# Expert layers: products of biases ahead of the tiles, first rows ahead of weights, outputs summed by TensorE

## The chip, the cores and the metric

The kernel runs on one core of one Trainium2 chip. The metric is device time in microseconds (us) of one launch. Before the change it is 1733.27 us, the median of three runs (1730.6 to 1735.8).

## The reference, cut to what matters

A decoder of four layers, each of a self attention, a cross attention and a feed-forward, each followed by a residual sum and a layer norm: `x = layernorm(x + sub(x))`. x has 8 batches of 112 rows of 256 values. The change lies in the feed-forwards of layers 0 and 1, which are mixtures of 8 experts (256 to 1024 to 256). Layer 0 weighs the best two experts of each row:

```python
logits = einsum('bsd,ed->bse', x, w_router)
top_vals, top_idx = top_k(logits, 2)
router_weights = softmax(top_vals)
h = gelu(einsum('eud,bsd->bseu', w_up, x) + b_up)
down = einsum('edu,bseu->bsed', w_down, h) + b_down
out = sum over the two picks of router_weights * down[pick]
```

Layer 1 scales the row by its gate `wi` ahead of expert i, and a row's output is that of the last expert with `wi > 0`, so only one expert's output counts per row:

```python
h = relu(xf * wi @ w1[i] + b1[i])
y = h @ w2[i] + b2[i]
out = where(wi > 0, y, out)
```

## The kernel before, in words

All is f32. The program of each engine is written out by hand, and semaphores order them. SUBS lists the twelve stages; `experts` is the part of stages 2 and 5 on TensorE (`pe`), VectorE (`dve`) and ScalarE (`act`), `expert_tiles` their part on SyncE (`sp`), `routed` theirs on GpSimd (`pool`). n is 0 for the first of these stages ("first layer" below) and 1 for the second ("second layer").

Routing gives each row a slot in DRAM (`slots`), in which rows of one expert stand together; GpSimd sends rows there with indirect DMAs (line 3865, semaphore `sent`), the last two batches of rows at the start of the stage. There are 21 tiles of 128 rows in the first layer and 14 in the second. A small `table` says which expert and which region of `slots` each tile has; SyncE loads both numbers into registers for each tile (`registers`, lines 685 and 686).

Per tile SyncE fetches a block of rows (`rows_to`, xrow, 128 KB), the up-weights (`up_weights`, wup, about 1 MB) and the down-weights (`down_weights`, wdn, 1 MB), three buffers each, and stores the outputs (yrow). Weights of tile 0 are fetched much earlier. For tile i + 3 the block of rows is issued after the down-weights of tile i + 2, which wait until the down-products of tile i - 1 are done. TensorE turns the rows (`turned`, line 2020), multiplies by the up-weights (`up`, line 2031, 32 records) and, after ScalarE's activation (line 2645), by the down-weights (`down`, line 2044, 16 records). A f32 matmul shows as two records. Its order is turned(0), turned(1), up(0), and then for each i: turned(i + 2), up(i + 1), down(i). VectorE copies turned rows and outputs out of the banks (lines 3555, 3571).

The bias of the down-products is not added per tile. For each batch of rows t, one matmul of the transposed gates (wtT) with the eight biases gives what all picks of a row add. `biases(t)` (line 2007) makes this product ahead of turned(t + 2), into the upper half of that tile's bank, and VectorE adds the residual to it (line 3565, into `acc`). So tiles 2 to 9 each carry one.

While TensorE waits for the first rows it runs fillers: `warm` (line 845) is one matmul of 256 columns, two records, whose result is not used. There are eight of them ahead of turned(0).

After the last tile GpSimd fetches each row's outputs back with indirect DMAs (line 4051, ygot: two per batch in the first layer, one in the second). VectorE multiplies them with their gates and adds them to `acc` (lines 3584, 3586; in the second layer one addition, 3589), takes the statistics of the norm (2723, 2726), the reciprocal (3575) and the normed rows (2732). ScalarE takes the root (2654). TensorE turns the normed rows (852), ScalarE copies them out (2171, 2663). `opening(sub, t)` on each engine is what the next stage starts between these batches: on TensorE the queries and keys (line 880, 16 records) at t = 3, the values (888, and a turn 1117 in the first layer) at t = 4, and in the first layer the second queries and keys at t = 5. Three fillers stand ahead of rows_t(6) and three ahead of rows_t(7).

Of the kernel before, what the change touches and what calls it, by code (L numbers as in the profile page):

```python
# [22 lines left out]
ALU = mybir.AluOpType  # L23
# [7 lines left out]
START = 64  # L31
# [126 lines left out]
class Ffn:  # L158
# [10 lines left out]
    Ffn("L0_ffn", dn=8),  # L169
    Turned("L1_attn", rope=True),  # L170
    Cross("L1_xattn", mask=True, joined=True),
    Ffn("L1_ffn", dn=8),
# [71 lines left out]
def decoder(nc, ctxT, mask, mask_keys, x, consts, ffn_small, packs, ring_dram, moe_up, moe_dn, out):  # L244
    ctx = ExitStack()
    with ctx:
# [52 lines left out]
        with ExitStack() as turn:  # L299
# [72 lines left out]
            xs = take(T, B, DM)  # L372
            lg = take(T, B, 8)
# [126 lines left out]
        mix_step = sem("mix_step")  # L500
# [117 lines left out]

        def route_bank(n, k):

            return bank[turn_banks(SUBS[4], "L", k, 0, 0)[1]] if n and k < 4 else bank[0]
# [29 lines left out]
        def _(sp):  # L651
# [25 lines left out]
            def expert_tiles(sub):  # L677
# [154 lines left out]
        def _(pe):  # L832
# [1152 lines left out]
            def experts(sub, router, bias):  # L1985
# [18 lines left out]
                def biases(t):  # L2004

                    g = tile_of(n, t + 2)
                    pe.matmul(bank[g % 2][0:T, DM:2 * DM], wtT[:, t * T:(t + 1) * T], f(bias, 8),
                              start=True, stop=True).then_inc(dn_ready, 1)

                def turned(i):  # L2010
# [37 lines left out]
                for _ in range(8):  # L2048
                    warm(bank[3], 256)
# [3 lines left out]
                for i in range(count):  # L2053
                    if i + 2 < count:
                        turned(i + 2)
                    if i + 1 < count:
                        up(i + 1)
                    down(i)
                for t in range(B):
# [3 lines left out]
                    rows_t(sub, t, t % 2, bank[t % 2])  # L2063
                    opening(sub, t)
# [648 lines left out]
        def _(dve):  # L2713
# [810 lines left out]
            def experts(sub, key):  # L3524
# [32 lines left out]

                turned_in(0)
                turned_in(1)
                for i in range(count):  # L3560
                    if i + 2 < count:
                        turned_in(i + 2)
                    if i < B:
                        dve.wait_ge(dn_ready, db + i + 1)
                        dve.tensor_tensor(acc[:, i, :], bank[tile_of(n, i) % 2][0:T, DM:2 * DM], x_res[:, i, :], ALU.add)\
                            .then_inc(dn_done, 1)
# [10 lines left out]
                mixed = Steps(dve, mix_step, 0, B)  # L3577
                for t in range(B):
                    if t >= 2:
                        dve.wait_ge(xln_ready, at(sub, "row", t - 2, 1))  # L3580
                        apart(dve)
                    dve.wait_ge(got_in[t % 4], 16 * (2 * sum(PICKS[:n]) + PICKS[n] * (t // 4 + 1)))
# [661 lines left out]
```

## Time and profile before

| what | value |
|---|---|
| median of three runs | 1733.27 us (1730.6 to 1735.8) |
| the profiled execution's own time | 1736.08 us |
| its span | 1734.3 us |
| mean granted clock of TensorE | 0.961 |
| busy: TensorE matmul, VectorE, ScalarE, GpSimd | 1529.8, 881.5, 646.6, 412.1 us |
| tiles of the first layer | about 364 to 526 us in the span |
| tiles of the second layer | about 857 to 968 us in the span |

How to read it: times are us from the start of the span, durations us unless marked ns. PE is TensorE's matmul and PEld its weight loads (which overlap), DVE is VectorE, ACT ScalarE, POOL GpSimd, SP SyncE; SPq and the like are an engine's queue. L2031 is line 2031 of the kernel. The granted clock is a share of 2.4 GHz: 1.00 is 2.4 GHz and 0.50 is 1.2 GHz, its other level. Names are tiles without buffer numbers: `bank` is PSUM, `route` holds acc and wtT, `arena` the routing's scratch among others.

### The profile page before, as it was taken

The page shows a single profiled execution, that of the slowest core. Times are in us where ns is not written, and L with a number is a line of the kernel's source. Part 1 is how long each engine was busy: PE and PEld are TensorE (multiplying, and loading weights), DVE is VectorE, ACT ScalarE, POOL GpSimd, SP SyncE. Part 2 cuts the span into 40 slices and gives each one's busy share as a digit, 9 for nine tenths or more (in the row PEclk, how much of TensorE's full clock was granted, in tenths as well). Part 3 has the DMA queues.
Part 4 walks back from the last instruction along what each step waited for, and adds up shares of the span by engine and source line. Part 5 has one row for each costly group of instructions (what it writes and reads, how often), then busy time and mean ns, then how long its engine had stood idle before and what let it go on. Part 6 is the DMA issues. An engine that isn't in the chain of part 4 may idle for free.

```text
span 1734.3 us, 39360 instructions
## 1 busy us (share of the span) xinstructions
PE 1529.8 (88%) x15024; PEld 1263.2 (73%) x15024; DVE 881.5 (51%) x2278; ACT 646.6 (37%) x1547; POOL 412.1 (24%) x627
## 2 busy tenths in 40 slices
PE   7998998889995888887799599997998999999998
PEld 6876777678994665565588477875786776789897
DVE  3665777521105555556311364567344555666764
ACT  3334876323332333444122323662663444311110
POOL 2224776610004331111100134552111111000101
PEclk9998999989997999999899799998999999999999
DMA  5443000178871002110588201101002000033332
GB/s 201 157 155 137 29 27 15 55 270 299 320 274 49 2 1 83 30 30 7 221 278 301 90 1 47 42 28 49 2 1 76 29 29 2 25 122 98 94 104 67
DMA packets 41984, 166.82 MB, mean 96 GB/s; under 512 B 6114, under 2 KB 16994, under 8 KB 30306
## 3 DMA queue, kind: packets, MB, share of 16 engines
q1 hardware_dynamic: 39522, 159.14, 26.5%
q0 software_dynamic: 2304, 5.51, 1.0%
q8 instruction: 106, 1.74, 0.4%
q14 instruction: 52, 0.43, 0.1%
HBM read 140.22 MB, written 24.41 MB: 95 GB/s over the span
## 4 chain that ended last, share of the span: by engine, by line
PE 67%; DVE 14%; issue 8%; POOL 4%; ACT 3%; DMA 3%; SPq 0%; DVEq 0%; POOLq 0%; ACTq 0%
PE bank L2031 7%; PE bank L2044 7%; PE bank L1973 4%; PE bank L1975 4%; PE bank L1974 4%; PE bank L1638 2%; PE bank L880 2%; PE bank L871 2%; PE bank L1658 2%; PE bank L845 2%; PE bank L1627 2%; PE bank L1401 2%; DVE big L3417 2%; PE bank L972 2%; DMA xrow<-slots 1%
## 5 line engine op out<-in xcount | busy, mean ns | idle before, releaser
L3708 POOL TENSOR_TENSOR mv<-mv,cst 112x1 f32<-112x1 f32 x88 | 20.8, 237 | 586.5 <-DVE mv L2726 586.5
L2645 ACT ACTIVATE htile<-bank,wup 128x128 f32<-128x128 f32 x280 | 79.8, 368 | 188.5 <-PE bank L2031 188.5
L2031 PE MATMUL bank<-xtile,wup 128*128 128x128 f32 x1120 | 135.2, 280 | 0.2
L2031 PEld LDWEIGHTS bank<-xtile,wup 128*128 128x128 f32 x1120 | 132.2, 197 | 1.1 <-DVE xtile L3555 1.0
L2044 PE MATMUL bank<-wdn,htile 128*128 128x256 f32 x560 | 126.3, 379 | 0.0
L3571 DVE COPY yrow<-bank 128x256 f32<-128x256 f32 x35 | 14.9, 425 | 217.2 <-PE bank L2044 217.2
L2044 PEld LDWEIGHTS bank<-wdn,htile 128*128 128x128 f32 x560 | 103.9, 190 | 12.7
L3882 POOL TENSOR_SCALAR arena<-arena,c_lo 112x375 f32<-112x375 f32 x64 | 98.0, 1544 | 33.8 <-ACT c_lo L2416 33.6
L2686 ACT ACTIVATE tmp<-bank,ffs 128x448 f32<-128x448 f32 x48 | 30.5, 635 | 182.8 <-PE bank L1975 182.7
L4051 POOL DMA_INDIRECT ygot<-slots,arena x24 | 22.9, 955 | 310.1 <-DMA slots<-yrow 300.2
L845 PE MATMUL bank<-ffs 128*128 128x256 f32 (+1 forms) x326 | 87.3, 413 | 2.1 <-ACT route L2636 2.1
L3417 DVE CUSTOM_DVE_ANT_0 big<-bank,big 112x375 f32<-112x375 f32 x128 | 62.6, 546 | 51.6 <-PE bank L1638 51.2
L2171 ACT COPY xT<-bank 128x224 f32<-128x224 f32 (+1 forms) x96 | 33.6, 350 | 145.0 <-PE bank L852 139.3
L2509 ACT ACTIVATE arena<-bank,arena 125x448 f32<-125x448 f32 x96 | 53.0, 635 | 79.5 <-PE bank L1658 79.5
L852 PE MATMUL bank<-cst,xln 112*128 112x112 f32 x176 | 37.2, 297 | 51.3 <-DVE xln L2732 44.5
L3420 DVE TENSOR_REDUCE arena<-bank 112x2 f32<-112x750 f32 x64 | 57.2, 936 | 40.2 <-PE bank L1638 40.1
L1638 PE MATMUL bank<-big,arena 32*112 32x375 f32 x512 | 57.6, 517 | 18.7 <-ACT arena L2509 13.5
L2412 ACT ACTIVATE arena<-big,nm 112x375 f32<-112x375 f32 x128 | 70.8, 603 | 8.7 <-DVE nm L3336 7.1
L845 PEld LDWEIGHTS bank<-ffs 128*128 128x128 f32 x326 | 63.3, 203 | 13.3 <-ACT route L2636 2.8
L852 PEld LDWEIGHTS bank<-cst,xln 112*128 112x128 f32 x176 | 22.8, 158 | 68.9 <-DVE xln L2732 53.8
L1401 PEld LDWEIGHTS bank<-cst,arena 112*125 112x125 f32 x384 | 49.5, 194 | 24.2 <-issue 9.1
L2511 ACT ACTIVATE arena<-bank 125x448 f32<-125x448 f32 x96 | 44.5, 550 | 58.9 <-PE bank L1658 58.4
(388 smaller groups left out, 3800.4 us busy)
## 6 DMA issues: line engine op xcount, KB each, us to landing
wup<-in_moe_up SPq DMA_DIRECT2D x35, 1028.0 KB, 7.3
wdn<-in_moe_dn SPq DMA_DIRECT2D x35, 1024.0 KB, 5.6
vspace<-in_ring SPq DMA_DIRECT2D x40, 512.0 KB, 4.1
ctxs<-parts SPq DMA_DIRECT2D x30, 564.0 KB, 3.7
slots<-mlpw SPq DMA_DIRECT2D x11, 1024.0 KB, 6.4
parts<-ctxs SPq DMA_DIRECT2D x8, 564.0 KB, 3.1
xrow<-slots SPq DMA_DIRECT2D x35, 128.0 KB, 4.9
slots<-yrow SPq DMA_DIRECT2D x35, 128.0 KB, 7.1
```

What stands on the lines that cost most here:

```text
L845: pe.matmul(out[:, 0:n], f("rhsT")[:, 0:128], f("rhsT")[:, 0:n], start=True, stop=True)
L1401: mm = pe.transpose(bank[4 + (3 * g + t) % 2][0:KT, j * T:(j + 1) * T], c_pr[:, g, j, t * KT:(t + 1) * KT], ident[0:T, 0:T])
L1638: mm = pe.matmul(out[i][0:T, 0:S2], c_qm[rows, p, g // 2, g % 2, :], c_kT[rows, p, g // 2, :], start=True, stop=True)
L1973: pe.matmul(out, weights[0], rows[0], start=start, stop=False)
L1974: pe.matmul(out, weights[0], rows[1], start=False, stop=False)
L1975: return pe.matmul(out, weights[1], rows[0], start=False, stop=stop)
L2031: mm = pe.matmul(bank[2 + 2 * (g % 2) + m // 4][:, m % 4 * ROWS:(m % 4 + 1) * ROWS], wup[:, g % 3, k * HID + 128 * m:k * HID + 128 * m + 1 ...
L2044: mm = pe.matmul(bank[6 + g % 2][:, 0:DM], htile[:, g % 2, k, :], wdn[:, g % 3, k * DM:(k + 1) * DM], start=(k == 0), stop=(k == 7))
L2412: nc.scalar.activation(c_pr[:, g, j, :], c_sc[:, g % 2, j, :], ACT.Exp, bias=nm[:, p, h:h + 1], scale=-1.0).then_inc(cexp_done, 1)
L2645: ins = nc.scalar.activation(htile[:, g % 2, m, :], bank[2 + 2 * (g % 2) + m // 4][:, m % 4 * ROWS:(m % 4 + 1) * ROWS], func, bias=wup[:, ...
L3417: ins = dve.tensor_tensor_reduce(c_sc[:, g % 2, i, :], bank[first + k][0:T, 0:S2], c_row[:, b % 2, :], 1.0, -LOWEST, ALU.add, ALU.min, j_m ...
L3882: ins = nc.gpsimd.tensor_scalar(c_pr[:, g, j, :], c_pr[:, g, j, :], c_lo[:, p, h:h + 1], 1.0, ALU.max, ALU.min)
```

## The change

- All eight products of biases move to the place ahead of the fillers, into banks that the first up- and down-products don't use yet (`bias_rows`); the fillers go from eight to four. VectorE adds the residual to four of them before its copy of tile 0's rows and to four after it. up(1) waits for all eight additions.
- SyncE now waits for the sends (`sent`) right after the registers of tile 0 and issues rows_to(0), then the registers of tile 1, up_weights(1), rows_to(1), down_weights(1), the registers of tile 2, rows_to(2), up_weights(2), down_weights(2). Before, the registers of all three tiles and both weights of tile 1 went ahead of the wait, and the three blocks of rows followed it together.
- After the last tile, TensorE sums the outputs: per batch it multiplies each ygot block and acc by the identity (in the first layer ygot by a diagonal matrix of gates, `mix`, that VectorE makes during the tiles) and accumulates in a bank, three banks in turn. Three batches go ahead of rows_t(0); the output of batch t + 3 stands between rows_t(t) and opening(t). VectorE reads statistics and normed rows out of that bank.

```diff
@@ expert_tiles (SyncE)
                 registers(0)
+                sp.wait_ge(sent, 16 * B * sum(PICKS[:n + 1]))
+                rows_to(0)
                 registers(1)
                 up_weights(1)
+                rows_to(1)
                 down_weights(1)
                 registers(2)
-                sp.wait_ge(sent, 16 * B * sum(PICKS[:n + 1]))
-                rows_to(0)
-                rows_to(1)
                 rows_to(2)
@@ experts (TensorE)
+                for t in range(B):
+                    pe.matmul(bias_rows(n, t), wtT[:, t * T:(t + 1) * T], f(bias, 8), start=True, stop=True).then_inc(dn_ready, 1)
...
-                    if 4 <= i < B + 4:
-                        pe.wait_ge(dn_done, db + i - 3)
-                    if 2 <= i < B + 2:
-                        biases(i - 2)
...
+                    if i == 1:
+                        pe.wait_ge(dn_done, db + B)
...
-                for _ in range(8):
-                    warm(bank[3], 256)
+                for _ in range(4):
+                    warm(bank[7 - (2 + 2 * (tile_of(n, 1) % 2))], 256)
...
+                def outputs(t):
+
+                    pe.wait_ge(got_in[t % 4], 16 * (2 * sum(PICKS[:n]) + PICKS[n] * (t // 4 + 1)))
+                    if t >= 3:
+                        pe.wait_ge(xln_ready, at(sub, "row", t - 3, 1))
+                    parts = [(mix[:, k, t, :] if n == 0 else ident[0:T, 0:T], ygot[:, t, k, :]) for k in range(PICKS[n])]
+                    parts.append((ident[0:T, 0:T], acc[:, t, :]))
+                    for k, (picks, rows) in enumerate(parts):
+                        mm = pe.matmul(bank[(2, 6, 7)[t % 3]][0:T, 0:DM], picks, rows, start=(k == 0), stop=(k == PICKS[n]))
+                    mm.then_inc(dn_ready, 1)
+
+                pe.wait_ge(edn_done, tile_of(n, count - 1) + 1)
+                for t in range(3):
+                    outputs(t)
                 for t in range(B):
...
                     rows_t(sub, t, t % 2, bank[t % 2])
+                    if t + 3 < B:
+                        outputs(t + 3)
                     opening(sub, t)
@@ experts (VectorE)
+                def biases_in(t):
+
+                    dve.wait_ge(dn_ready, db + t // 2 * 2 + 2)
+                    dve.tensor_tensor(acc[:, t, :], bias_rows(n, t), x_res[:, t, :], ALU.add).then_inc(dn_done, 1)
+
+                for t in range(4):
+                    biases_in(t)
                 turned_in(0)
+                for t in range(4, B):
+                    biases_in(t)
                 turned_in(1)
...
+                    for k in range(2 if n == 0 and i < B else 0):
+                        dve.tensor_scalar(mix[:, k, i, :], c("ident", T)[:, 0:T], gw[:, 1 + k, i:i + 1], None, ALU.mult)
...
-                    if n == 0:
-                        mixed(dve.scalar_tensor_tensor(out=acc[:, t, :], in0=ygot[:, t, 0, :], scalar=gw[:, 1, t:t + 1],
-                                                       in1=acc[:, t, :], op0=ALU.mult, op1=ALU.add))
-                        ins = dve.scalar_tensor_tensor(out=res[:, t % 2, :], in0=ygot[:, t, 1, :], scalar=gw[:, 2, t:t + 1],
-                                                       in1=acc[:, t, :], op0=ALU.mult, op1=ALU.add)
-                    else:
-                        ins = dve.tensor_tensor(res[:, t % 2, :], ygot[:, t, 0, :], acc[:, t, :], ALU.add)
-                    ins.then_inc(ln_dve, 1)
-                    stats(sub, t, t % 2, 0)
+                    stats_of(t)
                     if t:
                         inverse(t - 1)
-                        rows_out(sub, t - 1, (t - 1) % 2)
+                        rows_of(t - 1)
                     opening(sub, t)
```

`stats_of` and `rows_of` are the old steps with the bank in place of `res`.

## Rows read from the trace of the kernel before

**Rows 1.** The page: the chain that ended last, by engine.
```profile
PE 67%; DVE 14%; issue 8%; POOL 4%; ACT 3%; DMA 3%; SPq 0%; DVEq 0%; POOLq 0%; ACTq 0%
```
**Rows 2.** The chain in order of time, first layer: start, duration, what.
```profile
352.80 4.80 DMA slots<-x_res,arena
...
357.77 5.62 DMA xrow<-slots
...
371.93 3.57 PE bank L2031 x32
...
396.80 6.44 DMA xrow<-slots
```
**Rows 3.** Windows of one tile each: engines' busy time, granted clock, DMA share, GB/s.
```profile
420.35:428.35 8.00, 8.00 (x54) 6.96 (x54) 1.18 (x3) 2.28 (x8) 0.00 (x0) 1.00 0.82 296
428.35:435.60 7.25, 7.25 (x53) 6.79 (x52) 0.93 (x3) 2.28 (x8) 0.00 (x0) 1.00 0.95 327
```
**Rows 4.** Timeline, start of the first layer's tiles.
```profile
355.63 5.41 PE L845 MATMUL bank<-ffs 128*128 128x256 f32 x16 [1.03 <-ACT route L2636]
...
357.77 1.38 SPq L707 DMA_DIRECT2D xrow<-slots  x3
...
364.63 6.32 PE L2031 MATMUL bank<-xtile,wup 128*128 128x128 f32 x32
```
**Rows 5.** Windows of the fillers and of the first products, first layer.
```profile
355.60:361.04 5.44, 5.41 (x16) 4.14 (x16) 0.00 (x0) 0.00 (x0) 0.00 (x0) 0.69 0.93 342
...
363.43:370.90 7.47, 7.38 (x37) 6.83 (x37) 0.85 (x2) 2.39 (x5) 0.00 (x0) 0.57 0.67 280
```
**Rows 6.** Timeline, start of the second layer's tiles.
```profile
843.82 5.63 PE L845 MATMUL bank<-ffs 128*128 128x256 f32 x16 [1.03 <-ACT route L2636]
...
848.55 0.35 SPq L693 DMA_DIRECT2D wup<-in_moe_up  x1
...
857.80 5.54 PE L2031 MATMUL bank<-xtile,wup 128*128 128x128 f32 x32
```
**Rows 7.** Windows, same place.
```profile
847.00:849.00 2.00, 2.00 (x9) 1.73 (x8) 0.00 (x0) 0.00 (x0) 0.00 (x0) 0.82 0.00 0
...
853.00:855.00 2.00, 0.00 (x0) 0.00 (x0) 0.00 (x0) 0.00 (x0) 0.00 (x0) 0.89 0.99 414
```
**Rows 8.** Landing of xrow (first layer), wup (to 380), ygot (all), each from its own answer.
```profile
DMA to landing us min/median/max: 3.9/4.8/6.4
...
DMA to landing us min/median/max: 4.8/5.4/7.2
...
DMA to landing us min/median/max: 2.6/2.7/6.1
```
**Rows 9.** Timeline, end of the first layer.
```profile
530.04 0.94 POOL L4051 DMA_INDIRECT ygot<-slots,arena  x1 [0.30 <-issue]
...
532.70 0.48 DVE L3584 SCALAR_TENSOR_TENSOR route<-ygot,arena,route 112x256 f32<-112x256 f32 x1 [6.54 <-DMA ygot<-slots,arena]
...
545.85 3.62 PE L880 MATMUL bank<-xT,wat 128*128 128x112 f32 x16
...
552.73 2.04 PE L880 MATMUL bank<-xT,wat 128*128 128x112 f32 x16
```
**Rows 10.** Timeline, end of the second layer.
```profile
993.12 0.41 PE L852 MATMUL bank<-cst,xln 112*128 112x112 f32 x2
```
**Rows 11.** The chain: six and four records of 256 columns, and SP's first load.
```profile
554.77 1.31 PE bank L845 x6
...
813.30 2.05 PE bank L871 x4
...
845.99 0.45 SPq L685
```
**Rows 12.** One line's instructions: count, duration ns min/median/max, first and last start, forms.
```profile
L2723 DVE BATCH_NORM_STATS2 st<-res x104: 416/427/429, 55.0 to 1727.2; 112x6 f32<-112x256 f32 x104
...
L3565 DVE TENSOR_TENSOR route<-bank,x_res x16: 414/415/417, 372.3 to 920.8; 112x256 f32<-112x256 f32 x16
```

More of the change, by code:

```diff
@@ L168 @@
     Cross("L0_xattn", clip=True),
-    Ffn("L0_ffn", dn=8),
+    Ffn("L0_ffn", dn=16),
     Turned("L1_attn", rope=True),
     Cross("L1_xattn", mask=True, joined=True),
-    Ffn("L1_ffn", dn=8),
+    Ffn("L1_ffn", dn=16),
     Turned("L2_attn"),
@@ L372, in decoder @@
             xs = take(T, B, DM)
+            mix = xs.rearrange("p b n -> p (b n)")[:, 0:2 * B * T].rearrange("p (k t n) -> p k t n", k=2, t=B)
             lg = take(T, B, 8)
@@ L499, in decoder @@
         v_zero = sem("v_zero")
-        mix_step = sem("mix_step")
         rt_ready, rt_step, rt_exp = sem("rt_ready"), [sem("rt_step0"), sem("rt_step1")], sem("rt_exp")
@@ L617, in wait_turn, with bias_rows @@
                 eng.wait_ge(route_in, 6 * (sub.index // 3) + b + 1)
+        def bias_rows(n, t):
+            first = 2 + 2 * (tile_of(n, 1) % 2)
+            return bank[(first, first + 1, 6, 7)[t // 2]][0:T, t % 2 * DM:t % 2 * DM + DM]
         def route_bank(n, k):
@@ L2002, in experts @@
                 count = TILES[n]
[L2004 to L2008, printed above, removed]
+                for t in range(B):
+                    pe.matmul(bias_rows(n, t), wtT[:, t * T:(t + 1) * T], f(bias, 8), start=True, stop=True).then_inc(dn_ready, 1)
                 def turned(i):
@@ L3562, in experts @@
                         turned_in(i + 2)
[L3563 to L3566, printed above, removed]
+                    for k in range(2 if n == 0 and i < B else 0):
+                        dve.tensor_scalar(mix[:, k, i, :], c("ident", T)[:, 0:T], gw[:, 1 + k, i:i + 1], None, ALU.mult)
                     g = tile_of(n, i)
@@ L3575, in inverse, with sums @@
                     dve.reciprocal(mv[:, t % 2, 3:4], mv[:, t % 2, 2:3]).then_inc(ln_pool, 2)
-                mixed = Steps(dve, mix_step, 0, B)
-                for t in range(B):
[L3579 to L3582, printed above, removed]
-                    if n == 0:
-                        mixed(dve.scalar_tensor_tensor(out=acc[:, t, :], in0=ygot[:, t, 0, :], scalar=gw[:, 1, t:t + 1],
-                                                       in1=acc[:, t, :], op0=ALU.mult, op1=ALU.add))
-                        ins = dve.scalar_tensor_tensor(out=res[:, t % 2, :], in0=ygot[:, t, 1, :], scalar=gw[:, 2, t:t + 1],
-                                                       in1=acc[:, t, :], op0=ALU.mult, op1=ALU.add)
-                    else:
-                        ins = dve.tensor_tensor(res[:, t % 2, :], ygot[:, t, 0, :], acc[:, t, :], ALU.add)
-                    ins.then_inc(ln_dve, 1)
-                    stats(sub, t, t % 2, 0)
+                def sums(t):
+                    return bank[(2, 6, 7)[t % 3]][0:T, 0:DM]
@@ new lines, in stats_of, with rows_of @@
+                def stats_of(t):
+                    v = START + 3 * (sub.base["ln"] + t)
+                    dve.wait_ge(dn_ready, db + B + t + 1)
+                    dve.bn_stats(st[:, t % 2, :], sums(t)).then_inc(ln_dve, 2)
+                    dve.wait_ge(ln_dve, v + 2)
+                    apart(dve)
+                    dve.bn_aggr(mv[:, t % 2, 0:2], st[:, t % 2, :]).then_inc(ln_dve, 1)
+                def rows_of(t):
+                    dve.wait_ge(xt_ready, xt_at(sub, t) - 2)
+                    dve.wait_ge(xres_done, at(sub, "row", t, -1))
+                    dve.wait_ge(ln_pool, START + 2 * (sub.base["ln"] + t) + 2)
+                    dve.tensor_scalar(xln[:, t % 2, :], sums(t), mv[:, t % 2, 0:1], mv[:, t % 2, 3:4], ALU.subtract, ALU.mult)\
+                        .then_inc(xln_ready, 1)
@@ L3592, in experts @@
+                for t in range(B):
+                    stats_of(t)
                     if t:
                         inverse(t - 1)
-                        rows_out(sub, t - 1, (t - 1) % 2)
+                        rows_of(t - 1)
                     opening(sub, t)
                 inverse(B - 1)
-                rows_out(sub, B - 1, 1)
+                rows_of(B - 1)
+                dve.sem_inc(dn_done, B)
             def quantised(sub):
```

## The prediction

> **What bounds the kernel now.** I read the page of the profile first: TensorE holds 67% of the chain that ended last [rows 1], so what counts is where TensorE waits and what it does needlessly. Then the chain of waits through both expert stages. Each has three parts. It begins with a wait: first for the rows being sent (4.80 us), then for their coming back (5.62 us) [rows 2]. Then it is TensorE alone, tile after tile, with one wait for rows of 6.44 us among them [rows 2]. It ends, after the last tile, in fetches of the outputs and a norm per batch, mixed with the openings of the next stage. The windows of one tile each show the price of a bias directly: 8.00 us for a tile with one, 7.25 us for the next without, granted clock 1.00 in both, TensorE busy to the end of each and the DMA share at 0.95 or less [rows 3]. So the middle is bound by TensorE. The timelines at both starts show what surrounds the wait: eight fillers, 16 records in 5.41 and 5.63 us, then nothing until rows come [rows 4, 6].
>
> **The biases out of the loop.** Sixteen tiles (eight per layer) lose 8.00 - 7.25 = 0.75 us each [rows 3]: -12.0 us. DVE loses an addition per tile there and gains two small products per tile in the first layer; its busy time in a tile is 1.18 us of 8 [rows 3], so both are free. Up-products of tile 1 now wait for all eight additions; these run while TensorE waits for rows or works on tile 0.
>
> **The biases in the wait, first layer.** TensorE starts at 355.63 and now has eight bias pairs and four filler pairs, 24 records. The mean granted clock over the fillers was 0.69 [rows 5]: 38% of them at 2.4 GHz, about 0.6 us before a fall near 356.2 and the rest after a rise near 359.6, and 1.2 GHz between. A 256-column record takes 1.31/6 = 0.22 us at 2.4 GHz and 2.05/4 = 0.51 us at 1.2 [rows 11]. Some 9 records end by 359.6, the other 15 take 3.2 us: done at 362.8. (The gap is small against the bounds: all 24 at 1.2 GHz would take 12.3 us, all at 2.4 GHz 5.3.) The wait lasted until 357.77 + 5.62 = 363.4, so this is covered.
>
> **Rows ahead of weights, first layer.** Before, three blocks of rows were issued from 357.77 on [rows 4], behind the weights of tile 1, and the first took 5.62 us [rows 2]. Now row block 0 is issued with nothing ahead and should land like a gather, in 2.6 us [rows 8]: 360.1. But TensorE turns block 0 and block 1 before its first up-product, and block 1 still stands behind the up-weights of tile 1. These now move behind the wait for the sends, and behind two register loads (one pair about 1.1 us: in the second layer two pairs fill the time from 845.99 [rows 11] to the issue at 848.55 [rows 6]). So: sends done 357.3 to 357.6, up-weights issued near 359.2, landing 4.8 us later at the least [rows 8], block 1 about 0.3 behind: 364.3. Up-products start at 364.4 instead of 364.63 [rows 4]: -0.2 us. That step taken alone gives almost nothing here; the bounds are +1.0 (a landing near 5.4, the median of up-weights [rows 8]) and -1.5 (sends done 2 us earlier, because no weights share the queues).
>
> **The clock that follows.** Before, TensorE stood idle from 361.0 to 363.4. The mean of 0.57 from there to 370.9 says that it then ran at 1.2 GHz until about 369.9 [rows 5]; the first up-products took 6.32 us [rows 4], the next 3.57 us [rows 2]. Now only the 1.5 us from 362.8 to 364.3 are bare, with a turn in them. In the second layer's pause, which began at 843.82 + 5.63 = 849.45 [rows 6], the clock was still up until about 854.6 (0.89 over 853 to 855 [rows 7]). The bare time is shorter than either pause kept it. I take the full clock: -2.75 us. Bounds: 0 and -2.75.
>
> **The same at the second layer.** SP gets the table at 845.99 [rows 11]; no queue moves a byte from 847 to 849 [rows 7], so the sends were done by 847.2. Block 0 goes out near 847.4, not behind the weights as before; the up-weights of tile 1 near 849.0 instead of 848.55, since one issue stands ahead; block 1 near 849.6. Landing 4.8 after the weights plus 0.3: block 1 at 854.1. Fillers and biases, 24 records from 843.82 with the clock low until 847.7 (0.82 in that window [rows 7]), end at 851.2. So up-products start at 854.5 and not at 857.80 [rows 6]: -3.3 us. There the bare time is 2.6 us; I let the clock fall as before, the set taking its 5.54 us. Bounds: -2.0 (weights landing in 5.4, sends later), -5.7 (the clock stays up as well).
>
> The weights of tile 2 go out 3 us later than before at the first layer: the up-weights near 362.5, landing about 369.5 (7.2 at the most [rows 8]). They are wanted after two sets of up-products and one of down-products, not before 375: covered.
>
> **The end of each layer.** DVE gives up two operations per batch in the first layer, 0.48 us for one [rows 9], and one in the second. TensorE takes on three products, six records: 1.31 us at 2.4 GHz, 3.07 at 1.2 [rows 11]; four in the second. It waits in order: the output of batch t + 3 stands ahead of the opening after rows t. In the first layer POOL issues two fetches per batch, each 0.93 us with a 0.30 us gap, so the outputs of batch t arrive at 532.70 + 2.49 t [rows 9]; batch 6 at 547.6. TensorE does not get to the queries and keys of the next stage, now after the product of batch 6, before 548.9, against 545.85. They take 1.8 us at the full clock (before, 3.6 at the low one), ending 550.7 against 549.5. Then the product of batch 7 (arrived 550.1) stands in front of the values: 1.3 us less what values and turn gain from the clock. The second set of queries and keys starts near 554.7 instead of 552.73 [rows 9], and all behind it shifts: +2.0 us. Bounds: 0 and +5.
>
> In the second layer POOL is not the pace. Three products at the low clock (2.05 us each), then the full clock, as TensorE is busy throughout: rows 6 are turned at 993.0 instead of 993.12 [rows 10], and rows 7, 0.5 us earlier. I take -0.3; bounds -1.5 and +3.
>
> A rule that speaks against reading sums from PSUM: the rows show no such price, a norm's statistics take 427 ns out of SBUF, an addition with an operand in a bank 415 ns [rows 12]. The Trainium skill (Perfetto Trace Analysis, Optimizing Scalar/DVE Operations) gives a DVE operation about 60 ns of access time on SBUF and 125 ns on PSUM; by that the statistics and norms of 16 batches would cost 32 x 65 ns = 2.1 us. By the rows the sum has nothing for it.
>
> **The sum.** -12.0 (loops) -0.2 -2.75 (first start) -3.3 (second start) +2.0 (first end) -0.3 (second end) = -16.55. The blocks of rows are issued 1.8 us after a tile's products end and once took 6.44 us [rows 2]; at 7.25 us a tile that leaves 5.45 us, and the landings run 3.9 / 4.8 / 6.4 [rows 8]. One such stall: +0.8. So -15.8 us. The profiled execution took 1736.08 us for a span of 1734.3, and would take 1720.3; it lies 2.8 us above the median of the runs, 1733.27, on which the forecast is made: 1717.5 us.
>
> **Rivals.** (1) Rows too late at the shorter tile: if landings are near 6.4, each of 16 tiles waits 0.95 us, +15 us, and the loops keep their old pace: 1732. For it, the one wait in the chain; against it, TensorE is busy for all of a tile of 7.25 us [rows 3]. (2) Slower than before: TensorE stays at 1.2 GHz in the ends and becomes their bound. A batch of the first layer then costs 3.07 + 0.64 of turning = 3.7 us against 2.49, and its second set of queries and keys starts near 567 instead of 552.73, with fillers some 19 us in all; the second layer 13 us. Set against the 17.5 us that the sum gains without the ends: about 1748. It decides from about 23 us of loss on. Against it: TensorE, busy from 363.4 on, had 2.4 GHz again by 369.9 [rows 5], and here it would be busy from 532.7 on. (3) Better: sends done early, the clock kept at both starts, no loss at the first end: -23 us, 1710. (4) DVE pays for operands in PSUM, and its order is what both ends wait for: if each of the 32 operations grows from 427 ns to the 480 ns of its dearest neighbour there [rows 9, 12], 32 x 0.053 = 1.7 us, 1719.2. Against it stands the 415 ns row [rows 12]. The page named above is the one that speaks for this.
>
> **How the numbers follow.** Forecast 0.67; (1) 0.07; (2) 0.05; (3) 0.11; (4) 0.05; something unseen 0.05 (four fifths of it still faster). A difference under 0.3% (5.2 us) can't be told from none: (1) lies inside it, and the last fifth of the unseen. Faster 0.87, same 0.08, slower 0.05. The bounds of the terms, not all on one side, carry the forecast from 1712 to 1725; the range goes to 1711 and 1727, which leaves the far ends of (3), and (1) and (2), outside.
>
> **What would show it.** Right: tiles of 7.25 us from the first on; up-products from about 9 us after the fillers start in the first layer, at full clock (3.6 us); in the second, 3 us sooner after the table; the first block of rows landed well before its turn, the second the one waited for; six records of products per batch in the first end, and queries and keys 3 us later after the first fetch than before. Wrong: waits for rows in the tiles; a granted clock of 0.5 through the ends; TensorE held by fetches so that the next stage's openings come over 5 us late.

## The result, and the profile after

| | kernel before | changed kernel |
|---|---|---|
| median of the timed runs | 1735.75 us (1729.89 to 1744.48, 19 runs) | 1727.85 us (1719.81 to 1734.94, 19 runs) |
| ratio to before, with its 95% interval | | 0.9948 [0.9935, 0.9962], or -9.0 us [-11.3, -6.6] |
| span of the profiled run, granted clock | 1734.3 us, 0.961 | 1718.0 us, 0.970 |

The change is faster, by 9.0 us where the sum had 15.8; at 1727.85 us it ends just above the range. (The 9.0 us come from the ratio on record; the two medians lie 7.9 us apart. The kernel before also measured 2.5 us above the 1733.27 us on which the forecast was built.) Its profiled run, 1719.81 us, is the fastest of its 19, so the two profiles may not simply be subtracted: parts that the change does not touch took 1377.2 us before and 1372.9 here, and up to 1383.1 in the variants below. I therefore cut each profile at points that belong to the two expert stages. **Start**: from the end of ScalarE's second copy of the routing weights (TensorE's fillers or bias records begin there) to the first record behind the first set of up-products, so that a wait for the next block of rows between the two counts as start. **Loop**: from there to the beginning of VectorE's last copy of a tile's output. **End**: from there to the first scores of the next stage. In us:

| profile | start 1 | loop 1 | end 1 | start 2 | loop 2 | end 2 | all six |
|---|---|---|---|---|---|---|---|
| before | 15.30 | 154.85 | 32.63 | 19.49 | 104.45 | 30.42 | 357.14 |
| changed | 15.05 | 149.13 | 34.65 | 15.86 | 99.26 | 31.16 | 345.11 |
| changed, second profile (experiment 10) | 15.05 | 151.15 | 36.55 | 15.51 | 98.63 | 30.58 | 347.47 |

The stages give back 12.0 and 9.7 us, a mean of 10.8.

**The tiles.** Windows of one tile each in the changed kernel, first layer, the first among those that used to have a bias, the second not (columns as in [rows 3]):

```profile
400.50:407.75 7.25, 7.25 (x52) 6.79 (x51) 1.13 (x4) 2.28 (x9) 0.00 (x0) 1.00 0.93 329
430.00:437.25 7.25, 7.25 (x52) 6.79 (x51) 0.76 (x2) 2.28 (x9) 0.00 (x0) 1.00 0.92 305
```

Both are the 7.25 us of [rows 3]'s second row; TensorE is busy for all of it, and VectorE's two small products per tile (1.13 against 0.76 us) cost nothing. The waits of TensorE for rows between the tiles come on top: in this profile it sat idle for them 0.2 us in the first layer and 1.1 in the second, against 0.3 and 0.6 before. Counted as what the tiles took beyond 7.25 us (8.01 with a bias) it is 2.3 us over both loops, against 1.25 before.

**The first start.** Timeline of the changed kernel (start, duration, engine, line, what; [rows 4] answers to it):

```profile
353.85 6.68 PE L2010 MATMUL bank<-ffs,route 8*112 8x256 f32 x16 [1.03 <-ACT route L2652]
355.01 0.35 SPq L712 DMA_DIRECT2D xrow<-slots  x1
...
357.14 0.35 SPq L698 DMA_DIRECT2D wup<-in_moe_up  x1
...
357.68 0.50 SPq L712 DMA_DIRECT2D xrow<-slots  x1
...
360.45 3.78 PE L850 MATMUL bank<-ffs 128*128 128x256 f32 x8
...
364.03 0.89 PE L2018 MATMUL bank<-cst,xrow 128*128 128x128 f32 x4
...
365.18 3.84 PE L2031 MATMUL bank<-xtile,wup 128*128 128x128 f32 x32 [0.26 <-DVE xtile L3571]
```

The landings in that stretch, from the answer for `xrow`, microseconds:

```profile
DMA to landing us min/median/max: 2.0/3.3/4.5
```

Block 0 landed 2.0 us after its issue, block 1 4.5 us after 357.68, at 362.2. Neither is waited for: TensorE goes from bias records to fillers to turning without a gap, and it is TensorE that is late. The windows of the same stretch say why:

```profile
354.40:364.20 9.80, 9.80 (x24) 6.84 (x23) 1.51 (x4) 0.00 (x0) 0.00 (x0) 0.50 0.68 238
...
365.20:368.80 3.60, 3.60 (x32) 3.60 (x33) 1.57 (x5) 1.48 (x2) 0.00 (x0) 1.00 1.01 426
```

TensorE is busy for 9.80 of 9.80 us at a granted clock of 0.50, the 1.2 GHz level; only then does it rise. The up-products then take 3.84 us at 2.4 GHz instead of [rows 4]'s 6.32, but they begin 11.38 us after the copy instead of 9.05. Net: -0.25 us. (For 0.5 us after the records began the clock was still up: it fell at 354.4.)

**The second start.** The rows here are the answer to [rows 6]:

```profile
838.36 6.50 PE L2010 MATMUL bank<-ffs,route 8*112 8x256 f32 x16 [1.03 <-ACT route L2652]
...
844.79 3.78 PE L850 MATMUL bank<-ffs 128*128 128x256 f32 x8
...
850.32 0.44 PE L2018 MATMUL bank<-cst,xrow 128*128 128x128 f32 x2 [1.32 <-DMA xrow<-slots]
...
850.59 3.74 PE L2031 MATMUL bank<-xtile,wup 128*128 128x128 f32 x32
```

```profile
839.20:849.20 10.00, 9.80 (x24) 6.56 (x22) 3.28 (x14) 0.00 (x0) 1.34 (x2) 0.50 0.59 204
849.40:850.40 1.00, 0.08 (x1) 0.09 (x2) 1.00 (x5) 0.00 (x0) 0.00 (x0) 1.00 0.91 367
850.70:854.20 3.50, 3.50 (x34) 3.50 (x33) 0.51 (x2) 1.14 (x4) 0.00 (x0) 1.00 1.04 425
```

The same 10 us at the low clock, but here block 1 is later still: TensorE waits 1.32 us for it, the clock stays up over this wait, and the set takes 3.74 us and not 5.54. Net -3.6 us.

**The first end.** Timeline; [rows 9] answers to it:

```profile
522.27 0.94 POOL L4083 DMA_INDIRECT ygot<-slots,arena  x1 [0.30 <-issue]
...
538.30 1.12 PE L2067 MATMUL bank<-ygot,arena 112*112 112x256 f32 x4 [1.61 <-DMA ygot<-slots,arena]
...
541.24 1.94 PE L885 MATMUL bank<-xT,wat 128*128 128x112 f32 x16
...
547.00 2.04 PE L885 MATMUL bank<-xT,wat 128*128 128x112 f32 x16 [0.52 <-DVE arena L2932]
```

Counted from the second fetch (530.04 before, 522.27 here), the queries and keys begin after 18.97 us instead of 15.81 and last 1.94 instead of 3.62; the second set begins after 24.73 instead of 22.69, +2.0 us.

**VectorE reading PSUM.** Statistics and normed rows out of a bank (count, ns min/median/max), to hold against the 427 ns of [rows 12] and, for the normed rows, against the second fence, which is the same operation out of SBUF in the kernel before:

```profile
L3608 DVE BATCH_NORM_STATS2 st<-bank x16: 420/431/433, 528.0 to 977.0; 112x6 f32<-112x256 f32 x16
...
L3618 DVE TENSOR_SCALAR xln<-bank,mv x16: 542/543/545, 530.6 to 979.6; 112x256 f32<-112x256 f32 x16
```

```profile
L2732 DVE TENSOR_SCALAR xln<-res,mv x96: 403/412/892, 56.7 to 1729.1; 112x256 f32<-112x256 f32 x96
```

### The profile page after: what moved, and what is told of

Same layout as the page of the kernel before. It is cut to its first block, busy times and chain, and to the rows that moved or that the text cites. A ratio compares the mean times of both kernels' runs of the same rounds, so it can differ in the third digit from the quotient of the medians.

```text
span 1718.0 us, 39497 instructions
## 1 busy us (share of the span) xinstructions
PE 1535.2 (89%) x15088; PEld 1271.4 (74%) x15088; DVE 873.4 (51%) x2270; ACT 645.9 (38%) x1547; POOL 411.4 (24%) x627
## 4 chain that ended last, share of the span: by engine, by line
PE 67%; DVE 13%; issue 8%; POOL 4%; ACT 3%; DMA 3%; SPq 0%; DVEq 0%; POOLq 0%; ACTq 0%
PE bank L2031 7%; PE bank L2044 6%; PE bank L1978 4%; PE bank L1980 4%; PE bank L1979 4%; PE bank L1643 2%; PE bank L876 2%; PE bank L850 2%; PE bank L885 2%; PE bank L1663 2%; PE bank L1632 2%; PE bank L1406 2%; DVE big L3433 2%; PE bank L977 2%; PE bank L1393 1%
## 5 line engine op out<-in xcount | busy, mean ns | idle before, releaser
L2031 PE MATMUL bank<-xtile,wup 128*128 128x128 f32 x1120 | 130.9, 275 | 0.3 <-DVE xtile L3571 0.3
L2031 PEld LDWEIGHTS bank<-xtile,wup 128*128 128x128 f32 x1120 | 128.0, 192 | 0.6 <-DVE xtile L3571 0.5
L850 PEld LDWEIGHTS bank<-ffs 128*128 128x128 f32 x310 | 61.7, 209 | 11.9 <-issue 3.9
L876 PE MATMUL bank<-wat,big 128*112 128x256 f32 x192 | 56.1, 416 | 11.4 <-DVE big L2774 11.3
L2781 DVE TENSOR_TENSOR res<-bank,xb 112x256 f32<-112x256 f32 x64 | 27.0, 422 | 71.3 <-PE bank L876 33.4
```

The source lines that it names most:

```text
L850: pe.matmul(out[:, 0:n], f("rhsT")[:, 0:128], f("rhsT")[:, 0:n], start=True, stop=True)
L876: mm = pe.matmul(ps[0:T, DM:2 * DM], c_oT[:, k, :], wo[:, k, :], start=(k == 0), stop=(k == 1))
L2031: mm = pe.matmul(bank[2 + 2 * (g % 2) + m // 4][:, m % 4 * ROWS:(m % 4 + 1) * ROWS], wup[:, g % 3, k * HID + 128 * m:k * HID + 128 * m + 1 ...
```

## The experiments

The expectations name their theories by letters, and the letters do not mean the same throughout. In 1 to 4, **A** is that the first start fell short because its 24 records stay at 1.2 GHz, with the loops as forecast, and **B** that waits for rows ate the gain of the loops. In 5, 6 and 8, **A** is that records which use only 8 of the 128 rows (a bias product multiplies 8 rows by 256 columns) do not bring TensorE's clock back, however busy they keep it, and **C** that the operands have nothing to do with it. In 7 and 9 the rivals are about which transfer is waited for, and in 10 **B** is that the first profile was chance. Experiments 1 to 3 take one part of the change each. Where one profile is compared with another, each is a single execution.

**1. The biases alone.** Before, with the new bias records, four fillers, and the additions on VectorE; SP's order and the sums as before.

```diff
-                    if 2 <= i < B + 2:
-                        biases(i - 2)
+                for t in range(B):
+                    pe.matmul(bias_rows(n, t), wtT[:, t * T:(t + 1) * T], f(bias, 8), start=True, stop=True).then_inc(dn_ready, 1)
...
-                for _ in range(8):
+                for _ in range(4):
```

> Only the products of biases move ahead of the tiles (with four fillers in place of eight); the order of the transfers and the sums of outputs stay as before. Theory A, that the step which failed is the first start (24 records of 256 columns stay at 1.2 GHz there and TensorE comes later than the rows) and the loops gave what was forecast: the 16 tiles lose about 0.7 us each, -11 us; the first up-products of the first layer start 2.3 us later after the end of the routing's last copy than before, but take 3.8 us and not 6.3, so -0.2 us there; in the second layer the rows still decide, up-products start 14.0 us after the first bias, -2 us at most from the clock. Sum -11 to -13 us, ratio 0.993. Theory B, that waits for rows at the shorter tile took the gain in most executions: over 0.5 us of waits for rows in many of the 16 tiles, sum -3 to -7 us, ratio 0.997.

Measured: 1730.14 us (12 runs) against 1737.39, ratio 0.9964 [0.9943, 0.9985]. Loops 151.38 and 99.57 us, so -8.4 us and not -12; starts 15.10 and 19.14, ends 32.72 and 29.71. Tiles took 7.25 us with or without a former bias; six waits for rows, 3.0 us of idle time in all, stand between them, and the tiles took 4.9 us more than 7.25 us each, where before had 1.25. So the price of a bias was read rightly, and 3.6 of the 12 us, some 30%, come back as waits. The six parts together are 9.5 us shorter, between the two theories (A had 11 to 13, B 3 to 7); the time, -6 us, is nearer to B.

**2. The rows alone.** Before, with the new order on SP's queue.

```diff
                registers(0)
+                sp.wait_ge(sent, 16 * B * sum(PICKS[:n + 1]))
+                rows_to(0)
                 registers(1)
                 up_weights(1)
+                rows_to(1)
```

> Only the order of the first transfers changes. Both theories: the second block of rows lands 8.3 us after the routing's last copy in the first layer, 7.8 before, so nothing is gained there (0 to +0.5 us); in the second layer it lands 11.9 us after against 12.8, -1 to -1.5 us. Sum about -1 us, ratio 0.9994. The forecast had -3.5 us for this step in the two layers together.

Measured: 1735.87 us, ratio 0.9995 [0.9973, 1.0016], no difference that can be told. Its profile has starts of 12.64 and 17.22 us, 2.7 and 2.3 below before, where the expectation had nothing in the first layer and 1 to 1.5 in the second. In the first layer the up-products begin 8.97 us after the copy, only 0.1 earlier than before; the gain is the clock's, as their set takes 3.67 us. TensorE had waited longer than before for it:

```profile
365.85 0.44 PE L2020 MATMUL bank<-cst,xrow 128*128 128x128 f32 x2 [3.02 <-DMA xrow<-slots]
```

Before, with the same fillers, the clock fell at 363.0 in a wait of 2.39 us; here it stood at 1.00 through 3.02 us. So the length of a wait does not by itself decide it, and one profile does not say how often the clock holds. The new order itself, without the clock, is worth 0.1 + 1.9 us here. The interval reaches down to -4.7 us, so that it leaves room for these 2 us and hardly for the 4.9 of the profile; how many executions lose the clock in that wait no run shows.

**3. The sums alone.** Before, with the outputs summed by TensorE in three banks (`outputs`, `stats_of`, `rows_of` of the diff).

```diff
-                    if t >= 2:
-                        dve.wait_ge(xln_ready, at(sub, "row", t - 2, 1))
...
+                for t in range(3):
+                    outputs(t)
                 for t in range(B):
...
+                    if t + 3 < B:
+                        outputs(t + 3)
```

> Only the sums of the outputs move to TensorE. Theory A: the first end takes 2.0 us more, the second 0.8 us more, sum +2.8 us, ratio 1.0016. Theory B says the same; a loss of 5 us or more would say that in most executions the ends run at the low clock, which the one profile did not show.

Measured: 1738.26 us, ratio 1.0008 [0.9989, 1.0027]. Ends 34.77 and 30.57 us: +2.1 and +0.15. In its profile this part gains nothing at either end and costs about 2 us; the time can't tell it from nothing.

**4. Biases and rows, no sums.** Lines against the changed kernel.

```diff
-                parts.append((ident[0:T, 0:T], acc[:, t, :]))
...
+                mixed = Steps(dve, mix_step, 0, B)
```

> The change without the sums on TensorE. Theory A: -0.2 (first start), -3.5 (second start), -11.1 (loops), so -14.8 us, ratio 0.9915, and faster than the changed kernel by 2.8 us. Theory B: no better than the changed kernel, ratio 0.995.

Measured: 1728.33 us (9 runs), ratio 0.9942 [0.9913, 0.9971]. Starts 15.11 and 15.88, as in the changed kernel; ends 32.68 and 29.72, so that the sums cost the changed kernel 2.0 + 1.4 us beside it. The time can't tell the two apart: of the two theories it is nearer to B's 0.995 than to A's 0.9915.

**5. Bias records with 128 rows.** The changed kernel with its eight bias products made of the fillers' operands: same count, same 256 columns, 128 rows instead of 8, and so other values as well. It leaves the biases of the outputs out.

```diff
-                    pe.matmul(bias_rows(n, t), wtT[:, t * T:(t + 1) * T], f(bias, 8), start=True, stop=True).then_inc(dn_ready, 1)
+                    pe.matmul(bias_rows(n, t), f("rhsT")[:, 0:T], f("rhsT")[:, 0:256], start=True, stop=True).then_inc(dn_ready, 1)
```

> The changed kernel with the eight products of biases replaced by eight products of the same output shape whose operands have all 128 rows and not 8 (the biases are thus left out of the result). Looks at the first starts alone. Theory A, that records with 8 rows don't bring the clock up: the clock comes back earlier than the 10.2 us of low clock that the changed kernel shows, the 24 records end before the second block of rows lands (8.4 us after the routing's last copy), and the first up-products of the first layer start 8.8 to 9.6 us after it, not 11.4. Theory C, that the length of the low stretch has nothing to do with the operands: 11.4 again in the first layer.

Measured, one run: 1732.1 us, beside 1735.4 for before. Its timeline:

```profile
357.71 5.39 PE L2010 MATMUL bank<-ffs 128*112 128x256 f32 x16 [1.03 <-ACT route L2652]
...
362.94 1.89 PE L850 MATMUL bank<-ffs 128*128 128x256 f32 x8
```

The clock was at 0.50 only until about 361.6 and 1.00 behind it; the 24 records end 7.2 us after the copy instead of 10.4, and the first start is 12.66 us instead of 15.05. This is A and not C; that the values of the operands matter and not their rows is left open by this edit. Block 1 is then what TensorE waits for (1.42 us), as the forecast had it. In the second layer the faster records leave a bare wait of 4.61 us, the clock falls in it, the set takes 6.16 us and the start 18.48: in the changed kernel the slow bias records had been covering this wait.

**6. Fillers ahead of the bias records.** The changed kernel with the order of the two turned round.

```diff
+                for _ in range(4):
+                    warm(bank[7 - (2 + 2 * (tile_of(n, 1) % 2))], 256)
                 for t in range(B):
                     pe.matmul(bias_rows(n, t), ...
```

> The changed kernel with its four fillers ahead of the products of biases and not behind them. Theory A: the clock is low or falls again by the end of the biases, so the first set of up-products takes over 4.5 us in at least one layer (3.67 and 3.58 in the changed kernel), with the start 10 to 11.4 us after the copy. Theory C: same length of start as in the changed kernel, sets of 3.6 us in both.

Measured, one run: 1733.11 us. Its timeline and its windows (granted clock third from the right):

```profile
359.44 3.42 PE L850 MATMUL bank<-ffs 128*128 128x256 f32 x8 [1.04 <-ACT route L2652]
362.80 3.92 PE L2012 MATMUL bank<-ffs,route 8*112 8x256 f32 x16
366.64 0.69 PE L2020 MATMUL bank<-cst,xrow 128*128 128x128 f32 x2
```

```profile
360.20:362.80 2.60, 2.60 (x8) 1.59 (x6) 0.00 (x0) 0.00 (x0) 0.00 (x0) 0.50 0.17 52
363.20:366.40 3.20, 3.20 (x16) 2.45 (x15) 1.51 (x4) 0.00 (x0) 0.00 (x0) 0.99 0.65 211
366.70:368.50 1.80, 0.63 (x3) 0.23 (x2) 1.13 (x4) 0.00 (x0) 0.00 (x0) 0.50 0.99 356
```

The clock is back at the end of the fillers, the bias records run at it, and then it falls again near 366.7, at the end of the 3.92 us of 8-row records, in which TensorE had not stood still for a moment. The first start is 15.34 us, no better than with the old order, now because the up-products run at 1.2 GHz (5.87 us); they begin 9.6 us after the copy, a little sooner than A had. In the second layer the clock had fallen at 848.0, before the fillers; it stood at 0.50 through their 3.7 us and the 7.16 us of bias records behind them and rose only at 865.0, 4.6 us after the turning had begun. Its start there is 17.35 us, 1.5 more than the changed kernel's.

**7. The biases last.** Before, with the bias products and additions behind the last tile of a layer, where TensorE waits for the outputs anyway; eight fillers; the registers of tiles 0 and 1 first, then rows 0 and 1 together, then the weights; sums as before.

```diff
-                        dve.tensor_tensor(acc[:, i, :], bank[tile_of(n, i) % 2][0:T, DM:2 * DM], x_res[:, i, :], ALU.add)\
-                            .then_inc(dn_done, 1)
...
+                pe.wait_ge(eup_done, tile_of(n, count - 1) + 1)
+                for t in range(B):
+                    biases(t)
...
+                registers(1)
                 sp.wait_ge(sent, 16 * B * sum(PICKS[:n + 1]))
                 rows_to(0)
                 rows_to(1)
+                up_weights(1)
```

> The kernel before, with the products of biases after the last tile, in the pause before the first fetched outputs (7.1 and 9.3 us), eight fillers as before, the sums on DVE as before; SyncE loads the registers of tiles 0 and 1, waits for the sends, and issues both first blocks of rows ahead of all weights. Theory A: loops -9 us (what the two kernels without the sums showed), first start: up-products 6.0 to 6.5 us after the copy (9.05 before), their set 4 to 6.3 us, -2.5 to -5; second start: 9 to 9.5 us (14.03 before), set 5.5, -4.5; ends 0. Sum -16 to -18 us, ratio 0.990. Rival: up-weights of tile 1 now land last, and the second set of up-products waits for them: half of the gain of the starts is lost, ratio 0.993.

Measured: 1724.21 us (6 runs), ratio 0.9907 [0.9879, 0.9936]. Starts 11.76 and 15.55, loops 150.51 and 98.46, ends 33.04 and 30.49: all six 339.81. Up-products begin 6.19 us after the copy. Block 2 is now late: its turn in front of the second set waited 1.73 us in the first layer and 2.96 in the second, and these waits are part of the starts. The rival had expected the up-weights to be the late ones.

**8. The biases first, without fillers.** Biases as in the changed kernel, no fillers, both blocks of rows ahead of the weights, sums as before. The lines removed, against the changed kernel:

```diff
-                for _ in range(4):
-                    warm(bank[7 - (2 + 2 * (tile_of(n, 1) % 2))], 256)
```

> The products of biases ahead of the tiles as in the change, but no fillers behind them; registers and both first blocks of rows first as in the kernel above; sums on DVE as before. Theory A: first start: biases end 6.7 us after the copy at the low clock, up-products start at 7.4 and their set takes 6.3 at 1.2 GHz, -1.6 us; second start 9.3 plus 5.5 to 6.3, -4.3; loops -9; ends -0.3. Sum -15 us, ratio 0.991. Theory C: the clock is back for the first sets, 2.6 us less in each.

Measured: 1719.47 us (10 runs), ratio 0.9917 [0.9889, 0.9946]. Starts 12.94 and 15.07, all six 339.75, the same as experiment 7: late biases with fillers and early biases without can't be told apart. The window from 358.6 to 364.4, with nothing but bias records, has 5.80 of 5.80 us busy at 0.50; the turning and up-products, 128 rows each, begin at 364.52 and have 2.4 GHz from about 368.5, so that the set takes 5.15 us.

**9. The biases last, rows of tile 2 earlier.** Lines against experiment 7.

```diff
                 up_weights(1)
-                down_weights(1)
                 registers(2)
                 rows_to(2)
+                down_weights(1)
```

> The kernel of the late biases (products of biases after the last tile of a layer, eight fillers as before, both first blocks of rows ahead of the weights, sums left on VectorE), with one more move: the registers and the rows of tile 2 now go ahead of the down-weights of tile 1. In the run without this move the turn of block 2 waited 1.73 us for its rows in the first layer, and the interval from the first to the second set of up-products was 5.85 and 6.97 us. Theory A (what bounds the start is the landing of the blocks, in the order in which they are issued, once records with 128 rows bring the clock back): the wait of 1.73 us falls below 0.5, the interval goes to 5.2 or less in the first layer; the two layers' stages come to 337.5 to 338.5 us in place of 339.8; time about 2 us under the kernel with the late biases, ratio to the kernel before 0.990, and 6 to 8 us under the changed kernel. Rival C (all transfers of the start share one bandwidth, so a block moved ahead only trades places with weights): the wait for block 2 goes and one for up-weights or down-weights of tile 1 of the same 1 to 2 us comes; stages at 339.5 to 340.5, no difference to the late kernel.

Measured: 1716.33 us (6 runs) against 1737.84, ratio 0.9897 [0.9860, 0.9934]; the changed kernel ran on the same chip with 0.9954. Its timeline:

```profile
355.15 5.41 PE L845 MATMUL bank<-ffs 128*128 128x256 f32 x16 [1.03 <-ACT route L2634]
357.56 0.92 SPq L707 DMA_DIRECT2D xrow<-slots  x2
...
361.29 3.84 PE L2026 MATMUL bank<-xtile,wup 128*128 128x128 f32 x32 [0.30 <-DVE xtile L3553]
...
373.61 0.44 PE L2015 MATMUL bank<-cst,xrow 128*128 128x128 f32 x2 [1.24 <-DMA xrow<-slots]
...
854.54 0.44 PE L2015 MATMUL bank<-cst,xrow 128*128 128x128 f32 x2 [1.98 <-DMA xrow<-slots]
```

Starts 9.86 and 12.76 us, 5.2 and 3.1 below those of the changed kernel. The waits for block 2 went from 1.73 and 2.96 us to none and 0.65, so the two starts won 4.7 us over experiment 7. But block 3 is now waited for (1.24 us in the first layer, 1.98 in the second), the loops are 2.3 us longer and the ends 0.4: the six parts together are 337.80, 2.0 below experiment 7. That is the sum that A gave, while half of what the starts won only moved, as C has it, though to the next block and not to the weights that C named. In time the intervals of experiments 7 and 9 overlap; against the changed kernel on the same chip the ratio is 0.9897/0.9954 = 0.9943, 0.6% faster, with the two intervals just overlapping.

**10. The changed kernel again.** No edit.

> The changed kernel itself once more, beside the late biases on the same chip, for a second profile. Theory A (the first start is a fixed loss: eight pairs of bias records with 8 rows at the low clock): the 24 records again take 10.3 to 10.6 us from the end of the route's copy, the up-products start 11.3 to 11.5 us after it at the full clock, as in the first profile; the loops again show tiles of 7.25 us plus waits for rows, and these waits come anew: 1 to 4 us over both layers, so that the loops give back 8 to 11 of the 12.2 us. Time 1727 to 1729, ratio 0.993 to 0.997. Rival B (the first profile's start was chance, and the clock usually comes back near 4 us after the records begin): up-products 9 to 10 us after the copy, stages some 2 us shorter than 345.1.

Measured: 1729.03 us (12 runs), ratio 0.9954 [0.9929, 0.9980]. The first start is the same to the hundredth, 11.38 us to the up-products and 3.67 for the set, and experiments 1 and 4, which open with the same records, have 11.43: rival B, chance, falls. The loops gave 3.7 and 5.8 us this time, with waits for rows of 1.2 and 0.6 us. The first end took 36.55 us, 1.9 more than in the first profile: after a wait of 1.90 us for fetched outputs the clock fell, and the next products and the queries and keys began at the low level (2.60 us from 544.2 on at 0.50). In the first profile the longest such wait was 1.61 us, and the clock stayed at 1.00 from 528.6 to 547; that the length of the wait decides it is not shown.

## Why the prediction was wrong

The direction was right, and so was where each part gains or pays; the size was not, 9.0 us against 15.8, and at the first start the mechanism failed too. Of the 10.35 us between the forecast of 1717.5 and the measured 1727.85, 2.5 are the kernel before, which measured slower than its first three runs. Term by term, from the two profiles of the changed kernel:

- **Loops, -12.0 (+0.8 for one stall).** The 0.75 us per bias is exact: tiles of 7.25 us throughout. But the loops gave 10.9 and 9.5 us, and 8.0 to 10.5 in the seven other kernels without biases in the loop. Rival (1) was right in kind: rows of the next blocks are a little late at several tiles, 0.1 to 1.5 us each, not at one. As time beyond 7.25 us a tile they come to 2.3 and 3.7 us over both loops, of which before had 1.25. Mis-sized by 0.3 to 1.7 us.
- **First start, -2.95: the step that failed.** It is this sentence: "Some 9 records end by 359.6, the other 15 take 3.2 us: done at 362.8", with the full clock behind it. It took the clock's return from a trace in which the fillers used 128 rows, and applied it to records of which 16 use 8. But for their first 0.5 us they ran at 1.2 GHz to the end, which its own bound ("all 24 at 1.2 GHz would take 12.3 us") nearly had, and the remark in brackets passed over it. Measured, the 24 were done 10.4 us after the copy, where the sum had 7.2. Experiments 5 and 6 show that it goes with the 8-row records. The full clock for the set came true, and was paid for with up-products that began 2.3 us later than the old ones. Measured: -0.25. Mis-sized by 2.7 us, the largest of the terms. Block 1 landed 8.4 us after the copy, where the forecast had 8.7 (364.3 in the time of the profile before), so that nothing of it was the DMA's; in the second profile it landed at 9.2, still before TensorE was ready. The clock's rise for the set was expected because the bare time was short; in the runs it went with fillers standing last (with the order turned round, or without fillers, the set began at 1.2 GHz: 5.87 and 5.15 us in experiments 6 and 8).
- **Second start, -3.3.** Measured -3.6 and -4.0, a size that came out by luck, since two errors cancel: the up-products began 12.3 and 11.8 us after the copy and not 10.7 (block 1 landed 11.9 and 11.3 us after it, forecast 10.3), but the clock stayed up (sets of 3.74 and 3.84 us, not 5.54).
- **First end, +2.0.** +2.02 and +3.92. The steps came as written: fetches pace it, the queries and keys start 3.2 us later (3.05 forecast), the second set 2.0. The second profile shows that the clock can still fall between two late fetches.
- **Second end, -0.3.** +0.74 and +0.16, inside its bounds. What was missed: a fetch buffer is free only after TensorE's product and the statistics behind it. GpSimd's fifth fetch went out 9.13 us after the first (965.50 against 956.37), and 6.85 before. Three products at the low clock (1.17 + 1.06 us each) stand in that.
- **Rival (4), PSUM.** The statistics cost 431 ns out of a bank and 427 out of SBUF, as the rows had said; the normed rows 543 and 412. So 16 x 0.13 = 2.1 us more of VectorE in both ends, and the row that I had compared with (an addition, 415 ns) did not stand for this operation. The Trainium skill (Perfetto Trace Analysis, Optimizing Scalar/DVE Operations) gives every DVE operation 65 ns more for PSUM as engine-busy time, and says that the latency in a profile is about twice that; the trace agrees for the normed rows (131 ns) and not for the statistics (4 ns). The 2.1 us equal the 32 x 65 ns of the prediction by chance, 16 operations at twice the price. Whether the 131 ns are a fixed access or a slower pace for each value no run here tells, and how much of the 2.1 us lies on the path was not tried by itself.
- **Rivals (2) and (3)** did not come: in the first profile the first end ran at 1.00 from 528.6 to 547, and neither start kept the clock over its bias records.

With the profiles' terms the stages sum to -12.0 and -9.7. The timed -9.0 [-11.3, -6.6] and -8.0 hold the mean of these, -10.8, at their edge. What remains beyond that, 2 to 3 us, is within what the untouched parts vary between profiles (1372.9 to 1383.1 us) and stays open.

The range also was too narrow at its upper end: it let one stall of 0.8 us stand for all of rival (1). The bounds of the first start (+1.0 and 0) did hold that it could give nothing, but for late landings and a lost clock, not for slow records.

## What to carry to other kernels

Before work is moved into a wait as a replacement for fillers, ask whether it keeps the clock as they do: note how many rows its records use and how many would stand in a run. The trace of the kernel before could not have told: there the 8-row records stood in pairs among records of 128 rows, at 1.00. One trial with the records alone (experiment 1) shows it. Putting such work behind the last tile, with fillers kept in front of the products, did as well as putting it first without fillers (339.81 and 339.75 us), and the kernel with the shortest stages here (experiment 9) builds on the former; its last move was not tried on the latter. When a loop bound by TensorE gets shorter, expect part of the gain back as many small waits for its tightest transfer, and when a buffer's reader moves to another engine, follow who frees the buffer.

## What the hardware showed that was not expected

Back-to-back matmuls with 8 rows of 256 columns did not bring TensorE from 1.2 to 2.4 GHz here, nor hold it there. With 16 of them at the head of the first layer's tiles, the low level lasted some 10 us of work in five profiles of four kernels (the changed one, twice; experiments 1, 4 and 8), and rose only after records with 128 rows had run; with the same number of 128-row records (experiment 5) it lasted 3.4 us. In the second layer of these kernels it lasted 10 to 14 us. Put behind the fillers (experiment 6), they ran at 2.4 GHz in the first layer, which was lost as they ended, with no pause before; in the second they ran 7.16 us at 1.2 GHz. Experiments 5 and 6 are one profile each, and experiment 5 changed the operands' values with their rows. The Trainium skill (TensorE: Matmul & The Clock Gate, Part 1) says that activity on TensorE releases the lower clock and does not tell rows apart; by that alone the clock would have come back among the bias records, and the 9.80 us at 0.50 with TensorE busy for 9.80 speak against it.
